# First attention: turned pairs and row pairs of a step in turn, the weighted sum behind them

## The reference, cut to what matters

```python
x = x + 0.5 * L0_ffn(layernorm(x))
x = x + L0_attn(layernorm(x))          # this case: 2 x 1024 tokens, 16 heads of 16, rotary, causal
x = x + 0.5 * L0_ffn(layernorm(x))
x = x + 0.5 * L1_ffn(layernorm(x))     # 6 blocks
x = x + L1_attn(layernorm(x))          # 16 heads of 128, 4 key-value heads, causal
x = x + 0.5 * L1_ffn(layernorm(x))

def L0_attn(h):
    q, k, v = heads(h @ Wq.T), heads(h @ Wk.T), heads(h @ Wv.T)
    q, k = rotate(q), rotate(k)
    scores = q @ k.T / sqrt(16) + causal
    return merge(softmax(scores) @ v) @ Wo.T
```

## Time and profile before

| | us |
|---|---|
| median of 3 runs | 2702.96 (2702.65 to 2706.17) |
| the profiled execution's own time | 2706.19 |
| its span | 2704.4 |
| PE busy | 2529.6 (94%) |
| PE weight loads | 2111.9 (78%) |
| DVE busy | 1835.7 (68%) |
| ACT busy | 1394.1 (52%) |
| POOL busy | 395.6 (15%) |
| mean granted clock of PE | 0.974 |

### The profile page before, as it was taken

How to read it: one execution, slowest core, us unless ns; L and a number is a source line. 1 busy time by engine, 2 the same in 40 slices (tenths; PEclk the granted TensorE clock), 3 DMA queues, 4 the chain that set the end, 5 groups by cost and what they waited for, 6 DMA issues and landing times. The chain is left out here.

```text
span 2704.4 us, 49906 instructions
## 1 busy us (share of the span) xinstructions
PE 2529.6 (94%) x16744; PEld 2111.9 (78%) x16744; DVE 1835.7 (68%) x3996; ACT 1394.1 (52%) x2456; POOL 395.6 (15%) x302
## 2 busy tenths in 40 slices
PE   3987999869999999998999999999999999999999
PEld 3864445368888888887888888888877788888888
DVE  4665777457767767766776767767777677777773
ACT  3421554645555555554555545555555555555553
POOL 2022000011112222122010010010000222212220
PEclk9997989979999999999999999999999999999999
DMA  4045322000000000000000000000000000000000
GB/s 158 0 109 105 58 40 38 2 32 32 1 32 31 0 31 31 20 1 20 1 20 2 20 20 0 20 20 0 20 31 1 32 32 1 32 31 0 31 1 31
DMA packets 18955, 73.48 MB, mean 27 GB/s; under 512 B 3328, under 2 KB 8192, under 8 KB 15616
## 3 DMA queue, kind: packets, MB, share of 16 engines
q1 hardware_dynamic: 18816, 71.78, 9.5%
HBM read 61.02 MB, written 10.49 MB: 26 GB/s over the span
## 5 line engine op out<-in xcount | busy, mean ns | idle before, releaser
L357 PEld LDWEIGHTS ps<-w,hid 128*128 128x128 f32 x5376 | 699.2, 190 | 56.4 <-DVE rb L433 14.6
L357 PE MATMUL ps<-w,hid 128*128 128x256 f32 x5376 | 719.8, 283 | 2.1 <-DVE rb L433 1.5
L326 PE MATMUL ps<-xT,w 128*128 (+1 forms) x2688 | 704.6, 398 | 0.0
L510 DVE TENSOR_TENSOR hid<-gel,hid 128x512 fp32r<-128x512 f32 x448 | 403.5, 911 | 350.2 <-ACT hid L398 341.5
L392 ACT ACTIVATE gel<-ps,b 128x512 f32<-128x512 f32 x448 | 306.9, 686 | 554.5 <-issue 542.8
L326 PEld LDWEIGHTS ps<-xT,w 128*128 128x128 f32 x2688 | 479.3, 190 | 78.5
L873 PE MATMUL ps<-pT,v_sb 128*128 128x512 f32 (+3 forms) x1152 | 265.5, 360 | 12.8 <-DVE pT L997 12.8
L398 ACT ACTIVATE hid<-gel 128x512 fp32r<-128x512 f32 x448 | 272.9, 622 | 0.0
L847 PE MATMUL ps<-k_sb,q_sb 128*128 128x512 f32 (+3 forms) x1152 | 256.8, 357 | 5.4 <-DVE q_sb L1015 5.4
L1482 DVE TENSOR_REDUCE nmx<-ps 128x1 f32<-128x512 f32 (+3 forms) x384 | 196.1, 552 | 75.3 <-PE ps L1290 54.8
L947 ACT ACTIVATE pT<-ps 128x512 fp32r<-128x512 f32 (+3 forms) x384 | 178.4, 489 | 126.5 <-PE ps L860 105.9
(11 more groups left out here) (123 smaller groups left out, 2943.9 us busy)
## 6 DMA issues: line engine op xcount, KB each, us to landing
wraw<-in_wffn SPq DMA_DIRECT2D x12, 2048.0 KB, 7.7
wraw<-in_w_a SPq DMA_DIRECT2D x8, 1280.0 KB, 5.5
qk_dram<-rope_hl SPq DMA_DIRECT2D x16, 512.0 KB, 3.3
xT<-qk_dram SPq DMA_DIRECT2D x60, 128.0 KB, 6.6
xb<-in_wffn SPq DMA_DIRECT2D x2, 2048.0 KB, 14.5
q_own<-qk_dram SPq DMA_DIRECT2D x18, 128.0 KB, 5.6
k_own<-qk_dram SPq DMA_DIRECT2D x18, 128.0 KB, 7.4
x<-in_x SPq DMA_DIRECT2D x4, 512.0 KB, 5.6
```

Source lines behind the costliest of these rows:

```text
L326: last = nc.tensor.matmul(ps[:, HPS + j % 4, :], w[par][:, wp, 0, k * HIDDEN + j * PART:k * HIDDEN + (j + 1) * PART], xT[:, xp, k, bass.ds ...
L357: last = nc.tensor.matmul(y_ps[:, t, :], hid[:, hp, j % 4, t * PART:(t + 1) * PART], w[par][:, wp, 1, j * DIM:(j + 1) * DIM], start=j == 0 ...
L510: nc.vector.tensor_tensor(hid[:, 1, j % 4, :], gel[:, j % 4, :], hid[:, 0, j % 4, :].bitcast(f32), ALU.subtract).then_inc(low_done, 1)
```

## The change

In a step, PE's order was turned pair, turned pair, row pair, weighted sum, row pair. It is now turned pair, row pair, turned pair, row pair, weighted sum. What follows a step (J, N, C, E, O) keeps its place beside the row pairs and at the step's end; only N, which comes with the second row pair, is now ahead of the weighted sum.

```diff
@@ -1231,9 +1231,10 @@
                     todo.append(("N", GROUPS - 1))
 
             for i in range(steps + AV_LAG):
-                if i < steps:
-                    todo += [("T", i // len(TILE_STEPS), i % len(TILE_STEPS), p) for p in range(2)]
-                rows_beside(i, 0)
+                for p in range(2):
+                    if i < steps:
+                        todo.append(("T", i // len(TILE_STEPS), i % len(TILE_STEPS), p))
+                    rows_beside(i, p)
                 if i >= AV_LAG:
                     g, s = divmod(i - AV_LAG, len(TILE_STEPS))
                     todo.append(("A", g, s))
@@ -1246,7 +1247,6 @@
                             for n in range(4):
                                 late.setdefault(i + 2 + n // 2, []).append(("E", b, n // 2, n % 2))
                                 late.setdefault(i + 4 + n // 2, []).append(("O", b, n))
-                rows_beside(i, 1)
                 todo += late.pop(i, [])
             for i in sorted(late):
                 todo += late[i]
```

## The result

The changed kernel took 2766.02 us in the median of 4 runs (2758.79 to 2780.92), the kernel before 2704.57 (2702.65 to 2718.38): a ratio of 1.0242, 95% interval 1.0209 to 1.0276, slower by some 61 us. The forecast was 2727 us in a range of 2711 to 2745: the sign is right, the size is not. The profiled execution took 2766.69 us with a span of 2764.9, 60.5 us over the one before.

The account below looks back on a forecast made before the run. The prediction took PE and DVE taking turns over a three-bank ring to bound the first attention. From 2703 us, +16.5 for the order, -1 for waits at group starts and +8 for the clock gave 2727, range 2711 to 2745.

Parts of the forecast that it names:

- What moves, and where the time is lost: First attention: only PE's stream moves, DVE, ACT, POOL and SP keep their order; DVE runs dry once a step.
- The order's own term: Steps with row pairs: sum and turned pair share one gap, 0.26 us a step over 63 steps, +16.5 us.
- No switch cost: Turned pair to row pair shows no extra load; the rival with 0.19 us a step, +12, 2739 us, had chance 0.04.
- The clock, "+8 us": First attention: two more falls to half clock of the size seen, less a part, +8 us.
- The prediction's own sign of being wrong: Wrong if time at the half clock explains more than half of the difference.
- The second rival: PE's longer waits make the clock fall in most head groups; five more falls, 2746 us, chance 0.16.
- PE's longer waits: First attention: with 0.26 us more of waiting a step, more falls of the clock were expected, not fewer.
- At the half clock an order is worth nothing: In 13 half-clock steps PE goes on almost without a wait (19.71 of 20 us busy), so they add nothing.
- DVE's waits: First attention: DVE's waits for a row pair go up by about 0.26 us a step.
- The bounds: Clock term: from -11 us with no falls left to +105 with half clock throughout the clean 190 or so us.
- The same steps of other groups passed without one: Both falls came behind s8 and s9, yet 5 of 7 groups passed clean, counted against many more falls.

Follow-up runs that it names:

- e1: The changed kernel with the two matmuls of every second turned pair issued three times into the same banks; 2713.9 us, ratio 1.0042 to the kernel before.
- e10: The changed kernel with the two matmuls of every second turned pair issued twice; 2714.0 us, ratio 1.0061 to the kernel before.
- e2: The kernel before with the matmuls of every second turned pair issued twice; 2700.9 us, ratio 0.9986 to the kernel before.
- e5: The kernel before reordered to turned pair, row pair, sum, row pair, turned pair, with the last 16 steps kept; 2722.5 us, ratio 1.0064.
- e11: The kernel before with one more 128-column DVE reduction (0.25 us) in each of the 80 steps, PE's order untouched; 2732.0 us, ratio 1.0077.

## Why the prediction was wrong

- **What moves, and where the time is lost**: this was right. DVE, ACT and the later stages are unchanged, the loss is in the steps with row pairs.
- **The order's own term**: it was right in mechanism and nearly in size. Forecast 3.15 us a group of twelve, measured 2.9; the gaps of 1.43/1.82, 1.70, 1.94 and 2.33 us came out as 1.43/1.86, 1.73, 1.95 and 2.37. Against the forecast's +16.5 us, e1 and e10 less e2 show 13 to 20.
- **No switch cost**: the turned pair to the row pair is 0.35 us (300.67 to 301.02), as forecast; e5 leaves a small price of turned pairs apart, well under the 12 us of that rival.
- **The clock, "+8 us"**: this is the step that failed. e1 shows 52 us in all between the changed kernel with and without its long half-clock times. The prediction's own sign of being wrong, the half clock explaining more than half of the difference, came true. The second rival had the mechanism, but priced as five more falls of the size of those seen before, 2746 us, it was still short. The falls here are not more of the same length: there are five instead of three, and they last up to 65 us. That a fall would end as soon as before was assumed, and was wrong. The cause that the prediction named, PE's longer waits, is supported: with the waits filled by repeated matmuls the falls all but go (e1, e10), and with waits added by DVE alone they grow somewhat (e11). Why the falls last so much longer in the new order is not shown.
- **"At the half clock an order is worth nothing"**: this was wrong too. The row of PE's 19.71 busy of 20 us was of the old order. In the new order the row pair that stands behind a turned pair has to wait for DVE at the half clock as well, 1.78 us from row pair to row pair, and step s11 takes 4.98 us for 4.46. By the estimate above this term, put at nothing, is about 16 us. PE also works less densely while the clock is down; whether this is what keeps it down was not tested by itself.
- **DVE's waits**: they were forecast to grow by about 0.26 us a step and grew by 0.48, over steps at both clocks.
- **The bounds**: the ceiling worked out (+105 for half clock throughout) did contain the result, but the range reached only 42 us above the kernel before. "The same steps of other groups passed without one" was read as safety. It was none: the kernel before has falls that begin in the same step s9 as most of the changed kernel's, and its half-clock time differs from execution to execution, by 119 to 179 us over 23 of them.

## What to carry to other kernels

Where two engines hand banks to each other over a short ring, what counts is how the long instructions are spread between the handovers: the same work put into one gap costs what it lasts beyond the other engine's time, and this can be added up from the starts in a timeline to a tenth of a microsecond. Where the clock of PE already falls now and then, bound a new wait by the half clock for the whole stage before pricing it by its own length (here the changed kernel lost 61 us, and e11 only 23 at nearly the same group length), and look at the rows for what PE does at the lower clock in the new order, not the old. And try waiting per bank instead of per pair: it was worth more here (17 us) than any order.

## What the runs showed of the hardware that was not expected

- The lower clock can last while PE is almost never idle in the records: 60.53 of 64 us busy at a clock of 0.50 (367 to 431 us of the changed kernel), and 45.77 of 48 later.
- Matmuls that repeat finished work made the kernel 52 us faster (e1), with no change in the whole-clock group (35.1 us).
- 0.25 us of added DVE time a step, 20 us in 80 steps, cost 23 us in the median, and the time at the half clock rose in the median as well (191 us for 162 over the whole kernel), with PE's instructions untouched (e11).
- The falls mostly begin at one place, step s9 behind the narrow steps: three of five in the changed kernel, four of five in e11. In the steps right before a fall of the changed kernel PE was never idle for more than 0.74 us at a time.
